# Rotary products dealt out two, two, one, none over the units of a group, feed-forward jobs in its second half, and the second norm in two parts by tokens

## The reference, cut to what matters

```
xn = layernorm(x); s = attention0(xn); g = silu(ffn0(xn)); x = x + s * g
xn = layernorm(x); s = attention1(xn); g = silu(ffn1(xn)); x = x + s * g
```

## Time and profile before

| | |
|---|---|
| median of three runs | 951.91 us (949.71 to 954.62) |
| the profiled execution | 954.33 us, of which the span of its instructions is 952.5 us |
| busy in the span | PE 85%, DVE 65%, ACT 49%, POOL 33% |
| mean granted clock of the tensor engine | 0.933 of full speed |
| chain that ended last | PE 38%, POOL 20%, issue 17%, DVE 14%, ACT 6%, DMA 3% |

### The profile page before, as it was taken

One profiled execution on the slowest core, in us unless ns is written; L12 is line 12 of the kernel. 1 busy time (PEld: TensorE's weight loads), 2 busy tenths in 40 slices (PEclk: granted clock), 3 DMA queues, 4 the chain that ended last, 5 costly groups with the idle time before them and its releaser, 6 DMA issues.

```text
span 952.5 us, 12959 instructions
## 1 busy us (share of the span) xinstructions
PE 809.0 (85%) x4480; PEld 478.4 (50%) x4480; DVE 617.0 (65%) x1601; ACT 468.1 (49%) x948; POOL 314.9 (33%) x264
## 2 busy tenths in 40 slices
PE   2547397869999999969999999969999999969996
PEld 1325265645534656745534656744533656745533
DVE  3896667555985566555985566654986565654972
ACT  3555456214477665214477655224467666214464
POOL 0573857100202667200202668200201768200201
PEclk9877798879999999979999999979999999979998
DMA  7401001207200210008300211008300310007400
GB/s 230 119 24 36 17 6 44 69 13 213 64 3 28 74 56 23 2 13 211 66 3 29 74 50 29 1 0 207 82 2 23 80 29 1 2 0 199 91 2 23
DMA packets 54001, 53.25 MB, mean 56 GB/s; under 512 B 14512, under 2 KB 43568, under 8 KB 53936
## 3 DMA queue, kind: packets, MB, share of 16 engines
q1 hardware_dynamic: 51488, 49.70, 19.8%
q10 hardware_dynamic: 2128, 1.68, 0.6%
q0 software_dynamic: 320, 1.05, 0.4%
HBM read 39.00 MB, written 13.14 MB: 55 GB/s over the span
## 4 chain that ended last, share of the span: by engine, by line
PE 38%; POOL 20%; issue 17%; DVE 14%; ACT 6%; DMA 3%; SPq 2%; POOLq 0%; DVEq 0%; ACTq 0%
POOL region L565 8%; POOL region L561 7%; PE bank L969 6%; PE bank L1115 5%; PE bank L1103 4%; PE bank L864 4%; PE bank L1056 3%; PE bank L1088 3%; DVE mx L1441 3%; PE bank L1041 3%; PE bank L958 3%; PE bank L1093 2%; ACT region L814 2%; PE bank L898 2%; POOL w1T L591 1%
## 5 line engine op out<-in xcount | busy, mean ns | idle before, releaser
L1441 DVE TENSOR_REDUCE mx<-bank 128x1 f32<-128x512 f32 x256 | 162.8, 682 | 54.6 <-PE bank L1056 53.5
L864 PE MATMUL bank<-xnT,wrope 128*128 128x512 f32 x320 | 151.2, 614 | 19.9 <-ACT region L705 10.9
L565 POOL TENSOR_TENSOR region<-region 128x512 f32<-128x512 f32 x80 | 106.5, 1331 | 176.3 <-DVE region L1289 171.6
L814 ACT ACTIVATE region<-bank 128x512 f32<-128x512 f32 x256 | 136.3, 597 | 52.8 <-PE bank L1093 48.9
L722 ACT ACTIVATE region<-region,nb 128x128 f32<-128x128 f32 x256 | 81.6, 390 | 121.5 <-DVE nb L1296 121.2
L598 POOL TENSOR_TENSOR region<-region,bo_bc 128x256 f32<-128x256 f32 x16 | 11.7, 730 | 296.1 <-DVE region L1345 296.1
L561 POOL TENSOR_TENSOR region<-region,sin_sb 128x512 f32<-128x512 f32 x60 | 80.9, 1348 | 64.3 <-ACT region L705 64.3
L864 PEld LDWEIGHTS bank<-xnT,wrope 128*128 128x128 f32 x320 | 59.5, 198 | 82.7 <-issue 72.6
L898 PE MATMUL bank<-region 128*128 128x128 f32 x512 | 77.4, 298 | 27.3 <-POOL region L565 17.7
L898 PEld LDWEIGHTS bank<-region 128*128 128x128 f32 x512 | 66.0, 202 | 41.8 <-POOL region L565 21.3
L1088 PE MATMUL bank<-Qp,Kp 64*128 64x512 f32 x256 | 75.3, 464 | 7.3 <-ACT region L814 7.3
(11 more groups left out here) (132 smaller groups left out, 1331.0 us busy)
## 6 DMA issues: line engine op xcount, KB each, us to landing
wrope<-in_wrope SPq DMA_DIRECT2D x80, 128.0 KB, 2.1
scratch<-region SPq DMA_DIRECT2D x32, 256.0 KB, 3.7
Qp<-scratch SPq DMA_DIRECT2D x64, 128.0 KB, 3.7
Kp<-scratch SPq DMA_DIRECT2D x64, 128.0 KB, 3.8
X<-in_x SPq DMA_DIRECT2D x4, 512.0 KB, 3.9
scratch<-region SPq DMA_DIRECT2D x16, 128.0 KB, 3.5
out<-X SPq DMA_DIRECT2D x16, 128.0 KB, 2.1
VW<-v_rows SPq DMA_DIRECT2D x16, 102.0 KB, 2.8
```

Of the source, the lines that this page charges most:

```text
L565: nc.gpsimd.tensor_tensor(dst, dst, tiles(sw[:, r % 2, :], i), ALU.add)\
L814: nc.scalar.activation(P1[:, n % 8, :], turned_bank(n)[:, :], ACT.Exp, scale=SCALE1)\
L864: mm = nc.tensor.matmul(misc(b, name)[:, 0:width], lhs(c), xnT[:, c, :], start=(c == 0), stop=(c == DC - 1))
L1441: nc.vector.tensor_reduce(mx1[:, g % 2, column:column + 1], s_ring[m % 3][:, :], AX.X, ALU.max)\
```

## The change

Three things change.

1. `rope_at`: two, two, one and no rotary products in the four units of a group, instead of two, one, two, none. For batches 1 to 3 the feed-forward products follow a new list, `FFN_LATER`; batch 0 keeps the old one. On POOL the squares of the unit before now stand ahead of a unit's rotations.
2. Between the blocks, DVE scales, gates, adds and normalises tiles 0 and 1, then tiles 2 and 3. The chain `rsqrt` of the second norm runs twice. PE makes output products 0 and 1 after projection 1, and 2 and 3 after projection 3; then it turns half of the tokens, makes the half query and key products and one value product, and the same for the other half.
3. The jobs `xh`, `qk` and `v1` get fixed banks, among them the two score banks for `v1`.

```diff
+FFN_FIRST = [0, 0, 0, 2, 0, 1, 1, 2, 0, 1, 1, 2, 2, 2, 2, 0]
+FFN_LATER = [0, 0, 2, 2, 0, 0, 2, 2, 0, 0, 2, 2, 2, 1, 1, 0]
...
-    return [5 * (g + 1) + i for i in ((0, 1), (2,), (3, 4), ())[t]]
+    return [5 * (g + 1) + i for i in ((0, 1), (2, 3), (4,), ())[t]]
...
-PLACED = {"dup": (1, 2, 3, 4), "down": (3, 4, 1, 2), "mt": (2,)}
+PLACED = {"xh": (0,), "qk": (1, 2, 3, 4), "v1": (5, 6), "dup": (1, 2, 3, 4), "down": (3, 4, 1, 2), "mt": (2,)}
...
                 for s in range(NKV * TT):
+                    for kind, i in ffn_at(b, s - 1) if s else ():
+                        if kind == "up":
+                            squares(b, i)
                     for r in rope_at(s):
                         rotate(b, r)
...
+                misc_done(projected(1), ("proj", 1))
+                turn_outputs0(b, 1)
+                pe.wait_ge(ot_ready.sem, ot_ready.at(b, 2))
+                output0(0)
+                output0(1)
+                misc_done(projected(2), ("proj", 2))
+                misc_done(projected(3), ("proj", 3))
+                output0(2)
+                output0(3)
...
+                turn_half(b, 0)
+                pe.wait_ge(xnT_ready.sem, xnT_ready.at(b, DC + 1))
+                for j in range(4):
+                    qk_half(j, 0)
+                values1(0)
+                turn_half(b, 1)
+                pe.wait_ge(xnT_ready.sem, xnT_ready.at(b, DC + 2))
+                for j in range(4):
+                    qk_half(j, 1)
+                values1(1)
...
+                for h in range(2):
+                    pair = (2 * h, 2 * h + 1)
+                    for t in pair:
+                        gated_ffn(t)
+                    for t in pair:
+                        gate_of(b, 0, t, F[:, t, :])
+                    for t in pair:
+                        gated_attention(t)
+                    base = 2 * TT + RSQRT + h * (TT + RSQRT)
+                    for t in pair:
+                        row_stats(b, 1, t)
+                    dve.wait_ge(ln_step.sem, ln_step.at(b, base + 2))
+                    norm(b, 1, pair, base)
...
+                half_rows(0)
+                values1(0)
+                half_rows(1)
                 for j in range(4):
                     low_part(j)
...
+                values1(1)
```

More of the change, by code:

```diff
@@ L105, with ffn_at @@
 OT_UNIT = NKV * TT - 1
-FFN_PER_UNIT = [0, 0, 0, 2, 0, 1, 1, 2, 0, 1, 1, 2, 2, 2, 2, 0]
-def ffn_at(s):
-    n = sum(FFN_PER_UNIT[:s])
-    return [(("gate", "up")[k % 2], k // 2) for k in range(n, n + FFN_PER_UNIT[s])]
+FFN_FIRST = [0, 0, 0, 2, 0, 1, 1, 2, 0, 1, 1, 2, 2, 2, 2, 0]
+FFN_LATER = [0, 0, 2, 2, 0, 0, 2, 2, 0, 0, 2, 2, 2, 1, 1, 0]
+def ffn_at(b, s):
+    per_unit = FFN_LATER if b else FFN_FIRST
+    n = sum(per_unit[:s])
+    return [(("gate", "up")[k % 2], k // 2) for k in range(n, n + per_unit[s])]
 def rope_at(s):
@@ L625, in _ @@
                         ternary(TERN_ORDER[4])
-                    for kind, i in ffn_at(s - 1) if s else ():
-                        if kind == "up":
-                            squares(b, i)
                 if b == 0:
@@ L693, in xnT_copies @@
                         .then_inc(xnT_ready.sem, 1)
-                for c in range(DC) if layer == 0 else ():
+                for c in range(DC):
                     nc.scalar.activation(xnT_hi[:, c, :], misc(b, ("xt", 0, c))[:, :], ACT.Copy)\
@@ L944, in front @@
             def front(b):
-                turn_rows(b, 0)
+                turn_rows(b)
                 for r in range(5):
@@ L1016, in _, with qk_half, values1 @@
                     pe.wait_ge(f_part_act, 2 * N_F)
-                turn_rows(b, 1)
-                def qk_job(j):
+                pe.wait_ge(pt1_ready.sem, pt1_ready.at(b, NKV * TT))
+                pe.wait_ge(mx0_done.sem, mx0_done.at(b, NKV * TT * REP))
+                def qk_half(j, h):
                     w = (w1q_sb, w1k_sb)[j % 2]
-                    product(b, ("qk", j), lambda c: w[:, c, (j // 2) * P:(j // 2 + 1) * P])
-                for j in range(4):
-                    qk_job(j)
-                for j in range(2):
+                    if h == 0:
+                        misc_take(pe, b, ("qk", j))
+                    cols = slice(h * 256, (h + 1) * 256)
+                    for c in range(DC):
+                        mm = nc.tensor.matmul(misc(b, ("qk", j))[:, cols], w[:, c, (j // 2) * P:(j // 2 + 1) * P],
+                                              xnT[:, c, cols], start=(c == 0), stop=(c == DC - 1))
+                    if h == 1:
+                        misc_done(mm, ("qk", j))
+                def values1(j):
                     misc_take(pe, b, ("v1", j))
@@ L1217, in split_ffn1, with rsqrt @@
                     .then_inc(f_part, 1)
-            def rsqrt(src, scale, eps, signal, b, base):
-                v, h, a = (newton[:, n, :] for n in range(3))
-                y, ints = rstd[:, :], lambda ap: ap.bitcast(mybir.dt.int32)
+            def rsqrt(src, scale, eps, signal, b, base, tiles=slice(0, TT)):
+                v, h, a = (newton[:, n, tiles] for n in range(3))
+                y, ints = rstd[:, tiles], lambda ap: ap.bitcast(mybir.dt.int32)
                 chain = [
@@ L1385, in _, with gated_ffn @@
                         outputs0(b, (s - TT - 1) // TT)
-                for t in range(TT):
+                def gated_ffn(t):
                     src = misc(b, ("proj", t))
```

129 lines of the change are left out of this document (66 added, 63 removed).

## The result

The changed kernel takes 923.81 us (median of four runs, 921.10 to 925.05) against 953.26 us for the kernel before in the same session (949.71 to 954.72). The ratio is 0.9682, with an interval of 0.9656 to 0.9708: 29.5 us less in the medians, where 34.5 were forecast. The profiled execution took 921.1 us, with a span of 919.2 us and a mean granted clock of 0.955. Its span is 33.3 us shorter than that of the profile before (952.5).

What follows compares the result with a forecast made beforehand. PE was taken as the bound, stopping for late POOL rotations and for DVE's norm between blocks. Savings of 24.5 + 16.4 - 6.4 = 34.5 us gave 919.8 profiled, median 917 us; case range 908 to 925, widened 903 to 938.

Steps and rivals of the forecast that it cites:

- Part 1: Batches 1 to 3: PE's stops for POOL and a projection wait go, 18.1 us, with low clock 24.5; batch 0 nothing.
- Rival (a): Groups of batches 1 to 3: POOL is still late, only 0.78 us a batch gained there, 939 us; chance 0.13.
- Its two waits: PE's waits at the second group (1.10 us) and first projection (0.78 us) go in each of batches 1 to 3.
- The moves of part 2: Between blocks: up products start 8.9 us earlier, PE stops 4.9 us for dealt rows, score product moves from 440.9 to 436.9.
- What part 2 is worth: Split second norm, four batches: 16.4 us from earlier score products, less 6.4 us for low clock behind the new stop.
- The clock behind the stop: After the stop for dealt rows PE returns at half clock, costing 1.6 us each time, 6.4 us; bounds nothing to 4.5 a batch.
- the 4 us that I had named as a sign of being wrong: Behind the wait for dealt rows: the prediction is wrong if the clock stays low beyond 4 us.
- The gain itself: First score product of block 1 comes earlier by 4.0, 4.0, 4.6 and 3.8 us, 16.4 us over four batches.
- (c): Between blocks: transfers are hidden and PE's 8.9 us arrive whole, 24.5 + 35.6, 892 us; chance 0.04.
- (d): Slower: low clock holds through the lead stage, doubling its 21.4 us, 995 us; chance 0.03.
- (b): Low clock after the new stop lasts 9 us, 4.5 us lost a batch, 928 us; chance 0.13.
- (e): A smaller new wait in both parts, not placed, 940 to 950 us; chance 0.06.

Runs made afterwards that it cites:

- e1: Kernel before with only the new rope_at, the new feed-forward lists and the squares ahead of the rotations: 925.03 us, ratio 0.9712 to the kernel before.
- e9: Changed kernel with the old list of feed-forward jobs in all batches (FFN_LATER = FFN_FIRST): 936.70 us, ratio 0.9845 to the kernel before.
- e2: Changed kernel with the old rotary order, old feed-forward list and squares behind the rotations, keeping the split second norm: 951.72 us, ratio 0.9991 to the kernel before.
- e5: e2 plus 20 matrix products with unused results in each batch, in the stop before the first score product: 941.58 us, ratio 0.9883 to the kernel before.
- e4: Changed kernel plus 20 matrix products with unused results in each batch, behind the six first up products: 915.57 us, ratio 0.9599 to the kernel before.
- e11: Changed kernel with the edits of e6 and e7 and ten of e4's unused products: 913.98 us, ratio 0.9592 to the kernel before.
- e6: Changed kernel with the second norm's turned rows on bank 5 and value products on banks 0 and 6: 919.08 us, ratio 0.9647 to the kernel before.
- e12: Changed kernel with e6's banks, eight up and 12 down products before the first scores, six down behind each pair: 909.20 us, ratio 0.9545 to the kernel before.
- e8: Changed kernel with the first deal issued from two queues, queries by SyncE and keys by ScalarE: 927.62 us, ratio 0.9731 to the kernel before.
- e10: e8 plus a wait, so the second deal starts when the first has landed: 924.58 us, ratio 0.9714 to the kernel before.
- e7: Changed kernel with eight instead of six up products ahead of the first score product: 919.10 us, ratio 0.9641 to the kernel before.

## Why the prediction was nearly right, and where it was not

**Part 1** was right in mechanism and size: T to P of batches 1 to 3 lost 24.6 us in the profile, 24.5 forecast, and nothing in batch 0 (0.7 longer). e1 measured 27.8 in the medians. Rival (a), POOL still late, is out. What I under-priced is the new feed-forward list. Its two waits I gave 1.10 and 0.78 us a batch; e9 shows it worth 4.2 (12.6 over three). It also clears the second unit ahead of the fifth rotary product. My sum has that product end at 13.3 us because it takes the second unit without a feed-forward product; I never priced this apart, and e9's expectation, 5.6 us, leaves it out. The forecast of part 1 as a whole does not suffer from it.

**The moves of part 2** were right too, in batch 1 that I had worked out. Counted from the first projection of batch 1, the forecast had the up products at 34.6 us and the score product at 47.4; they came at 34.62 and 47.75, with a stop of 5.19 us (forecast 4.9). The score product gained 15.0 us over four batches in the profile, 16.4 forecast. Batch by batch it is 6.7, 3.7, 4.1 and 0.5 us, against 4.0, 4.0, 4.6 and 3.8: batch 0 gave 2.7 us more than forecast and batch 3, with the bank wait and a low clock, 3.3 less. That the sum is close is luck.

**What part 2 is worth** was wrong in the medians. I netted 10.0 us, 16.4 less 6.4. The profiles of before and after give 15.0 less 5.6, which is 9.4. The medians give 1.2 us, both alone (e2 against before) and on top of part 1 (the changed kernel against e1; 2.9 by the ratios), each within its interval of nothing. So the term that was mis-sized is part 2's net, and the pair of profiles alone would have called it right. Of its two terms the runs show this:

- The clock behind the stop, forecast as 6.4 us (1.6 a batch). Counted from the score product the low clock lasts 3.4, 3.9, 3.4 and 4.6 us in the profile after, and S to T is 1.5, 1.7 and 1.5 us longer in batches 0 to 2: the price from the earlier trace rows holds there. The medians want more: filling the stop brought 8.2 us in the changed kernel and 10.1 in e2. In e2's profile the low clock behind the stop lasts 4.1 to 5.4 us in batches 0 to 2, and T to P of the later batches has two more low stretches of 3.4 us than before, which e5's has not; why a stop moves the clock so much later I can't say. The fourth low stretch, 4.6 us, is beyond the 4 us that I had named as a sign of being wrong.
- The gain itself, 16.4 us. With the low clock filled away, part 2 is worth 12.1 us alone (e5) and 9.5 on top of part 1 (e4 against e1). Much of what part 2 gains from P to S is clock: that stretch has 47.8 us at 1.2 GHz before, over four batches, and 8.6 after. How much differs from profile to profile: P to S is 4.8 us shorter in e1 than before, with the same code there. What part 1 already took of it, part 2 can't bring again.

The rule that I named, the Trainium skill's, TensorE: Matmul & The Clock Gate, "HAM oscillation — how this bites in real kernels", describes a kernel whose waits for transfers bring the clock down at every tile. The trace agrees: all four stops of 4.8 to 5.2 us have a low stretch behind them, and e4 removes them. e11 adds that a stretch with PE busy 73% of 3.19 us, none of its waits over 0.55 us, was followed by one as well.

**The rivals.** (c) is out, since the stop for the dealt rows is there, and so is (d): the longest low stretch behind a stop is 6.8 us. (b) is out by its size: it wanted 9 us of low clock behind each stop, and there are 3.4 to 4.6. Only the time, 923.8 us, lies between the forecast and its 928. (e), a new wait not placed, did come, as the bank wait below, but not at its 940 to 950.

**Slips in the sums.** By the terms given, (b) comes to 929 us and (d) to 997. The bounds named (7 us in batch 0, the clock at nothing and at 4.5 us a batch, the dealt rows at 436.3 and 437.8), all taken together, give 901 to 932, so the range 908 to 925 is narrower than they are. None of this moves the forecast.

**What I missed** is the bank wait of e6: 4.7 us in the medians, of which the trace shows 2.5 us of waiting and, in the last batch, a low stretch behind it. I had followed the banks in batch 1 alone, the one batch without the wait.

So the forecast of 34.5 us came within 5 us of the 29.5 measured by two errors that offset each other: in the medians part 2 lacks 8.8 us (the bank wait among them) and part 1 gave 3.3 more, which the sum had nowhere. (These leave 5.5; the kernel before ran 0.4 us faster beside e1.) That part is luck. The profiles alone would have hidden this. Their spans differ by 33.3 us, since the changed kernel's is from the fastest of its four runs (921.1) and that of before lies near its slowest (954.3). Part of such spread comes from the start: the first rotary product waits for a copy on ACT, which stands behind the splitting of a weight piece, and that piece's transfer ends at another time in each profile. Timeline of ACT in e2 (in the changed kernel this row starts at 13.82, with a wait of 1.19):

```profile
17.04 1.06 ACT L659 ACTIVATE w1T<-th 128x1024 bf16<-128x1024 f32 x1 [4.05 <-DMA th<-in_wp]
```

## What to carry to other kernels

When a wait is removed, follow what is released to the next thing it has to meet, and price the stop that it makes there with the clock behind it: part 2's wait of 6.5 us became one of 5 us, and that left almost nothing in the medians until the stop was filled. A stop whose end is set mostly by bytes in flight was here best filled with work that is due later anyway (e12: 14.6 us with e6's banks, 9.9 of them over e6), and not attacked at the issue (e8: 3.8 us slower; e10: no change). And follow fixed resources such as banks through every repetition of a loop, since a rotation that does not divide evenly makes each repetition another case.

## What the runs showed of the hardware

- 20 matrix products more in each batch, 4.48 us of PE's time, made the kernel 8.2 us faster, because they stood in a stop of 5 us.
- Stops of 2.2 to 2.6 us (e7) were followed by more low clock than the stops of 5 us, about 35 against 19 us in S to T. The score products behind them have nothing in between; with down products between them (e12) no batch has low clock between its first score product and its last down product.
- Two queues that issue at once landed a deal of 1 MB later than one queue did (8.25 against 7.05 us) while the next deal ran beside it, with the DMA engines full (share 0.99 from 422.00 to the score product). With the next deal held back it took 6.9 to 7.7 us, of which 5.41 of 7.70 us in batch 1 moved bytes.
